# Attention scores and row maxima in one instruction stream: runs of 3, 3 and 2 pairs, one reduction over two PSUM banks for every other turn, and a lead of 28 turns in place of 30

## The reference

```python
q, k, v = (proj(wq, bq), proj(wk, bk), proj(wv, bv))
scores = jnp.einsum('bhqd,bhkd->bhqk', q, k) * scale
attn = jax.nn.softmax(scores, axis=-1)
out = jnp.einsum('bhqk,bhkd->bhqd', attn, v)
...
x = _layernorm(x + attention(x), axis=-1)
h = silu(tlin(x, w1)) * tlin(x, w2)
h = gelu(tlin(h, h1)); h = gelu(tlin(h, h2))
x = _layernorm(x + tlin(h, w3), axis=-1)
```

## Time and profile before

| what | value |
|---|---|
| median of 3 runs | 443.17 us (443.12 to 443.28) |
| span of the profiled execution | 441.5 us, first to last instruction |
| share of the span, PE / DVE / ACT / POOL | 97% / 88% / 83% / 20% |
| TensorE's granted clock | full speed in all 40 slices |

### The profile page before, as it was taken

The page is one execution under the profiler, slowest core; times in us unless marked ns, Lnnn a source line. Parts: engine busy times, 40 slices in busy tenths (PEclk is TensorE's granted clock), DMA queues, the critical chain, the costliest instruction groups (busy, mean ns, idle before and its releaser), DMA issues.

```text
span 441.5 us, 9824 instructions
## 1 busy us (share of the span) xinstructions
PE 427.8 (97%) x3496; PEld 227.0 (51%) x3498; DVE 386.5 (88%) x719; ACT 367.7 (83%) x694; POOL 90.3 (20%) x142
## 2 busy tenths in 40 slices
PE   8999999999999999999999999999899899999995
PEld 4543544444444444444444443544333488877884
DVE  6799999999999999999999999999884577657636
ACT  4487989998998999989899899999899886678762
POOL 9730000100000010000001002373311263046103
PEclk9999999999999999999999999999999999999999
DMA  6567741111130110113011001021021000000101
GB/s 165 176 196 129 270 147 33 44 28 28 48 122 25 45 31 28 27 48 122 25 46 33 26 27 49 14 43 47 15 39 50 13 8 1 1 2 2 48 1 48
DMA packets 17117, 24.88 MB, mean 56 GB/s; under 512 B 5169, under 2 KB 9009, under 8 KB 16689
## 3 DMA queue, kind: packets, MB, share of 16 engines
q1 hardware_dynamic: 16464, 23.68, 19.3%
q10 hardware_dynamic: 608, 0.59, 0.5%
HBM read 15.08 MB, written 7.60 MB: 51 GB/s over the span
## 4 chain that ended last, share of the span: by engine, by line
PE 76%; DVE 10%; ACT 5%; SPq 3%; DMA 2%; issue 2%; POOL 0%; POOLq 0%; DVEq 0%; ACTq 0%
PE ps L1369 24%; PE ps L1291 20%; PE ps L1479 16%; DVE negmax L977 9%; PE ps L1353 8%; ACT arena L664 2%; DMA parts_q<-arena 2%; PE ps L1223 2%; PE ps L1234 1%; PE ps L1423 1%; PE ps L1319 1%; PE ps L1263 1%; SPq L463 1%; SPq L435 1%; ACT v_pad L722 1%
## 5 line engine op out<-in xcount | busy, mean ns | idle before, releaser
L977 DVE TENSOR_REDUCE negmax<-ps 128x1 f32<-128x512 f32 x458 | 275.8, 701 | 1.8 <-PE ps L1291 1.5
L664 ACT ACTIVATE arena<-ps 128x512 f32<-128x512 f32 x360 | 190.0, 606 | 19.3 <-PE ps L1353 14.1
L1353 PE MATMUL ps<-qx,kx 64*128 64x512 f32 x512 | 171.3, 451 | 0.9 <-DMA qx<-mT 0.6
L1291 PE MATMUL ps<-kx,qx 61*128 61x512 f32 x468 | 160.2, 441 | 0.6 <-DMA qx<-parts_q 0.5
L1291 PEld LDWEIGHTS ps<-kx,qx 61*128 61x128 f32 x468 | 75.1, 184 | 88.6 <-DVE negmax L977 79.3
L1369 PE MATMUL ps<-arena,v_pad 128*32 128x256 f32 (+3 forms) x1328 | 104.8, 407 | 2.8 <-ACT arena L664 2.8
L664 ACT ACTIVATE hf<-ps 128x512 f32<-128x512 f32 x152 | 83.2, 604 | 9.4 <-PE ps L1353 8.4
L1353 PEld LDWEIGHTS ps<-qx,kx 64*128 64x128 f32 x512 | 78.9, 184 | 18.6 <-ACT arena L664 11.8
L1479 PE MATMUL ps<-hid,w_high 128*128 128x512 f32 (+1 forms) x296 | 68.3, 388 | 0.8 <-issue 0.4
L1479 PEld LDWEIGHTS ps<-hid,w_high 128*128 128x128 f32 x296 | 54.2, 188 | 12.3 <-issue 0.8
L1369 PEld LDWEIGHTS ps<-arena,v_pad 128*32 128x32 f32 x1328 | 28.5, 108 | 37.1 <-issue 30.7
(11 more groups left out here) (107 smaller groups left out, 317.2 us busy)
## 6 DMA issues: line engine op xcount, KB each, us to landing
qx<-parts_q SPq DMA_DIRECT2D x60, 64.0 KB, 2.1
late_sb<-in_late SPq DMA_DIRECT2D x3, 1280.0 KB, 5.5
kx<-parts_k SPq DMA_DIRECT2D x56, 64.0 KB, 2.2
parts_q<-prt SPq DMA_DIRECT2D x3, 512.0 KB, 6.4
parts_q<-arena SPq DMA_DIRECT2D x3, 512.0 KB, 8.3
xT_sb<-in_xT SPq DMA_DIRECT2D x4, 256.0 KB, 4.2
xT_sb<-arena SPq DMA_DIRECT2D x28, 32.0 KB
prt<-den SPq DMA_DIRECT2D x7, 128.0 KB
```

Of the source, the lines that this page charges most:

```text
L664: nc.scalar.activation(probs(n // HG)[:, heads(n), :], ps[:, PLAN["score", n][0], :], ACT.Exp, scale=SCALE).then_inc(exp_done, 1)
L977: nc.vector.tensor_reduce(negmax[:, t // TURNS % 2, m % 2, h * QT + q:h * QT + q + 1], ps[:, MAX_BANK + m % 4, :], AX.X, ALU.max, negate=T ...
L1291: nc.tensor.matmul(ps[:, half_bank(m), :], qx[at, slot, qc, h, q * P:(q + 1) * P], kx[at, slot, h, part * C:(part + 1) * C], start=True, s ...
L1353: nc.tensor.matmul(ps[:, bank, :], kx[at, slot, h % PAIR, kt * P:(kt + 1) * P], qx[at, slot, qc, h % PAIR, :], start=True, stop=True)\
```

## The change

Runs get three, three and two pairs in turn, so that three runs make eight pairs and two whole steps. On VectorE, the two halves of every even turn are reduced by one operation over two banks (`turn_both`), the halves of odd turns by one each as before. LEAD goes from 14 to 12: 25 turns in place of 27 in the beginning, and maxima 28 turns ahead of the scores. Plans that depend on run numbers are worked out from the new sizes.

```diff
-LEAD = 14
+LEAD = 12
...
-RUN_COLS = C * RUN // HG
-RUNS = (2 * U_ALL * TURNS - AHEAD + RUN - 1) // RUN
-TAIL = (RUN * (RUNS + RUN_BEFORE)) // HG
+PAIR_COLS = C // HG
+RUN_SIZES = (RUN, RUN, RUN - 1)
+BEFORE = RUN * RUN_BEFORE
...
+def run_at(g):
+
+    if g < 0:
+        return RUN * g
+    return g // len(RUN_SIZES) * sum(RUN_SIZES) + sum(RUN_SIZES[:g % len(RUN_SIZES)])
...
+def run_of(i):
+    return next(g for g in range(-RUN_BEFORE, i + 1) if run_at(g + 1) > i)
...
+RUNS = run_of(2 * U_ALL * TURNS - AHEAD - 1) + 1
+TAIL = (run_at(RUNS) + BEFORE) // HG
 GROUPS_ALL = RUNS + STEPS_ALL - (TAIL - 1)
-TURN_AT = {min((2 * TURNS * (w + 1) - 1 - AHEAD) // RUN + 3, RUNS + 1): w for w in range(1, U_ALL)}
+TURN_AT = {min(run_of(2 * TURNS * (w + 1) - 1 - AHEAD) + 3, RUNS + 1): w for w in range(1, U_ALL)}
...
-    return range(AHEAD + RUN * g, min(AHEAD + RUN * (g + 1), 2 * U_ALL * TURNS)) if g < RUNS else range(0)
+    return range(AHEAD + run_at(g), min(AHEAD + run_at(g + 1), 2 * U_ALL * TURNS)) if g < RUNS else range(0)
...
-    c0, c1 = RUN_COLS * g, RUN_COLS * (g + 1) if g < RUNS - 1 else (TAIL - 1) * C
+    c0, c1 = PAIR_COLS * run_at(g), PAIR_COLS * run_at(g + 1) if g < RUNS - 1 else (TAIL - 1) * C
...
+            def turn_both(i, m):
+
+                dve.wait_ge(max_scores, i * (2 * PER * TURNS) + m + 2)
+                t, bank = m // 2, MAX_BANK + m % 4
+                h, q = head_of(t % (PER * TURNS) + PER * TURNS)
+                nc.vector.tensor_reduce(negmax[:, t // TURNS % 2, 0, h * QT + q:h * QT + q + 1],
+                                        ps[:, bank:bank + 2, :], AX.XY, ALU.max, negate=True)\
+                  .then_inc(max_taken, 2)
...
                 for m in range(m0, m1):
-                    turn_half(i, m)
+                    if m % 4 == 0:
+                        turn_both(i, m)
+                    elif m % 4 > 1:
+                        turn_half(i, m)
```

More of the change, by code:

```diff
@@ L98, in scores_of @@
     if g < RUNS:
-        return range(RUN * (g + RUN_BEFORE), min(RUN * (g + RUN_BEFORE + 1), TAIL * HG))
+        return range(run_at(g) + BEFORE, min(run_at(g + 1) + BEFORE, TAIL * HG))
     k = g - RUNS + TAIL - 1
@@ L209, in half_bank @@
 def half_bank(m):
-    return MAX_BANK + (m + 2 * (FOLD // 2 + 1) if m < 2 * FOLD else m) % 4
+    return MAX_BANK + (m + WHOLE + 4 - FOLD if m < 2 * FOLD else m) % 4
 def build(nc, xT, wqT, wkT, wvT, woT, bq, bk, bv, bo, late,
@@ L283, in probs @@
             if k >= TAIL:
-                return probs_2[:, (k - TAIL) % 2]
+                return probs_2[:, (k - TAIL + TAIL % 3) % 2]
             return hf if k % 3 == 2 else probs_2[:, k % 3]
```

## The result

The changed kernel takes **458.48 us** (median of four runs, 456.98 to 461.05) against 443.14 us beside it: 1.0354 times as long (95% interval 1.0317 to 1.0390). The forecast of slower held; its 449.5 us and its range up to 454.5 us did not. The profiled execution took 456.98 us, its span is 455.2 us, 13.7 more than before.

The account below looks back on a forecast made before the run. VectorE bounds the kernel before; TensorE would bind after, at 19.70 us a unit. 13.44 units give +6.1 and the transposition +0.2, so 443.2 + 6.3 = 449.5 us, range 442.5 to 454.5.

Parts of the forecast that it names:

- TensorE passes VectorE: Main stretch: TensorE's unit rises from 18.8 to 19.40 us before late releases, above VectorE's 18.76 after the change.
- the short run: TensorE's third run of each block, with two pairs: takes 1.23 us, against 1.69 and 1.72 for three pairs.
- the unit's start: First product of a unit waits for ScalarE's copy and exponential: 0.58 us on TensorE, now in every unit.
- the transposition: Once a unit on TensorE it adds 0.26 us; at the end, up to 0.2 us behind the wait it stood in.
- the lead: Beginning: two folded turns less buy nothing, the score of unit 1 still waits until 56.23; four more halves remain.
- Every sign: Profile after: VectorE idle 0.2 us per block, blocks 4.7 to 4.8 and 5.2, record 1.22, first score 56.2, end 3.2.
- 13.44 x 19.70 = 264.8 against 258.7: Main stretch: units to go times us per unit, against the stretch measured before: +6.1 us, 2.4 from four further halves.
- of oddments: Main stretch: 0.14 us a unit, as VectorE has now, counted only in the upper bound of 20.05 a unit.
- The late release: Merged reduction frees its bank late for the next run's second pair: 0 to 0.17 us, taken as 0.10, 0.3 a unit.
- The end is the last reduction plus a constant: From last reduction through `norm` to `out_proj` and behind it nothing changes, except up to 0.2 us for the transposition.
- VectorE stays the bound: Rival for the main stretch: TensorE's unit falls below some 18.9, giving -4.5 us, 438.7 us; chance 0.15.
- The merged reduction costs its whole 1.225: Rival: no overlap, so VectorE keeps 19.5 a unit, 19.9 to 20.1 with unit starts; 452 to 454.7 us; chance 0.15.

Follow-up runs that it names:

- the runs alone: Changed kernel with LEAD back at 14 and every half reduced by itself, so only the 3, 3, 2 run plan differs from the kernel before: 447.44 us, 1.0102.
- the wait filled: Changed kernel with nine small identity matmuls while TensorE waits for `norm` ahead of `out_proj`: 456.68 us, 1.0302.
- the copy behind the exponential: Changed kernel with ScalarE's copy of a finished unit put behind the first exponential of the next run: 459.16 us, 1.0369.
- the merge in the first run: Changed kernel with LEAD 14 and merged reductions only in the first run of each block of eight pairs: 451.02 us, 1.0191.
- lead alone: Kernel before with LEAD 12 in place of 14, runs of three pairs and no merged reductions: 447.11 us, 1.0104.
- the kernel with the old lead: Changed kernel with LEAD put back from 12 to 14, keeping runs of 3, 3, 2 and merged reductions: 451.00 us, 1.0175.
- the two with half of the merges: Changed kernel with LEAD 14, merging only in each block's first run (451.02 us) or only in its second (447.72 us).

## Why the direction was right and the size was wrong

**Right.** TensorE passes VectorE: shown by the idle times and by the runs alone, whose pace (19.39) is the forecast's sum for TensorE without late releases (19.40). The parts of it in the changed kernel: the short run 1.23 (1.23 forecast); the unit's start 0.61 a block (0.58), now in every unit; the transposition 0.17 (0.26), since its block takes 4.97 against 4.80. The merged reduction has a record of 1.218 us and the next one begins 1.13 behind it (153.04 and 154.17). The rows of unit 1 landed at 56.15 (before 56.23), its first score began at 56.29, and the lead bought nothing in front. From the last maximum to `out_proj` it was a constant. Every sign that the prediction named came true: blocks of 4.80 and 5.25, a record of 1.22, 56.2 and 3.2.

**The step that failed** is the sum "13.44 x 19.70 = 264.8 against 258.7". The measured stretch is 270.99 us (56.15 to 327.14), 6.2 more. Of these, 4.8 are a comparison of unlike things and 1.5 a term that was too small.

- **A clean unit was set against a mean that wasn't clean.** At its pace of 19.22 the 13.31 units of before make 255.9 us, so the 258.7 hold 2.8 us of disturbances, 1.4 of them in the three late units. The 264.8 hold none; 0.14 a unit "of oddments" stood in the upper bound alone. The measured stretch is 4.8 us above 13.44 units at 19.81 (266.2): 2.8 in the three late units; 1.1 at the end, where 8 halves take 6.10 us and 8/32 of 19.81 is 4.95, since the unit's start among them makes a run of 2.84 in place of 2.33; and 0.8 in front, where 6 halves, from 56.15 to the copy of unit 0, take 4.54 and the pace gives 3.71, since the run that waits for the rows is held up. Even had all disturbances stayed as before, the stretch would have been 2.8 above the sum; that they grew by 2.0 was foreseen by no step.
- **The late release: "I take 0.10, between the ends".** It is 0.16 three times a unit, 0.48 in place of 0.30. The step before it was already wrong: by its own figures the load is 2.12 - 1.80 = 0.32 late and the matmul 2.12 - 2.03 = 0.09, and "0 to 0.17" follows from neither. The measured load is 0.32 late (0.43 behind the run's start in place of 0.11). A unit is then 18.56 + 0.48 + 0.61 + 0.17 = 19.82, measured 19.81, and not 19.70. That makes the 1.5 us.
- **"The end is the last reduction plus a constant."** The constant held up to `out_proj`. Behind it the forecast had 0.2 us for the transposition, and it is 1.5 us more.

**What no step had.** The prediction saw that one step leaves the wait for `norm`, and counted it as neither won nor lost. It made TensorE idle for 2.66 us there, and the clock behind that is 1.1 of the 1.5 us; that it is the idle time is shown by filling it. These terms (6.2 in the stretch, and 1.5 in place of 0.2 behind `out_proj`) lead from 449.5 to the profiled run's 456.98. The last 1.5 us are in the median: the other three runs of the change have mean clocks of 0.992, 0.986 and 0.992 against the profiled run's 0.995, and lie up to 4.1 above it. With the wait filled all four have 0.998 or 0.999 and lie within 1.1 us. But the four runs with the copy behind the exponential, whose wait is not filled, all have 0.992 and lie within 1.4, so why the change's runs spread so far is not shown.

**The rivals.** "VectorE stays the bound" is out: it idles 11.3 us in the main stretch. "The merged reduction costs its whole 1.225" is out by the 1.13, though its figure, 452 to 454.7, was nearer than mine, by luck: its reason did not hold. The rule of grouping on a saturated engine (the Trainium skill, Perfetto Trace Analysis, Optimizing Scalar/DVE Operations) was tested where it should be at its best, in the kernel before with a merge in twelve halves: the operations did get cheaper, by 0.07 to 0.09 a merge, and the kernel got slower. By the page's figure (an estimate) it would have been 0.125. The same section's other sentence, that breaking up may help where an unsaturated engine makes bubbles on another, agrees with the merge in the first run: without it the pace falls from 19.73 to 19.40.

**What stays open.** How much of the late units' loss goes if the weight work is moved away from the splits. What the other 0.4 us behind `out_proj` are, the moved transposition or something else: the runs alone have them too (123.78 against 123.34), at full clock. And no kernel has the new runs and 28 turns of lead without a merge.

## What to carry to other kernels

When two engines are both within a few per cent of full, work out the pace of each in a clean period, and compare clean with clean; put the disturbed periods and the ends in as terms of their own. An operation that takes two buffers at once starts later and gives both back later, so its price is in its neighbour's waits: look at who asks for the first of these buffers next, and merge only where that one comes late anyway (here the second run, at no cost, and no gain). And a fixed cost per group of work (here 0.31 us for each run: three pairs take 1.69 us and two take 1.23, so a pair 0.46, and 1.69 - 3 x 0.46 is left) is paid again for every group that a neater plan adds. Look also at what else is placed by counting such groups, as the weight work is here: it moves with them.

## What the runs showed of the hardware beyond what was expected

**TensorE's clock behind a wait of 2.7 us.** In six kernels, TensorE's idle time in front of `out_proj`, the mean granted clock from 320 to 340 us, and from `out_proj` to the end:

| kernel | idle before `out_proj` | clock | `out_proj` to the end |
|---|---|---|---|
| before | 0.86 | 1.00 | 123.34 |
| runs alone | 0.56 | 1.00 | 123.78 |
| lead alone | 2.68 | 0.91 | 124.86 |
| changed | 2.66 | 0.91 | 124.86 |
| changed, copy behind the exponential | 2.67 | 0.83 | 125.8 |
| changed, wait filled with matmuls | 0.48 | 1.00 | 123.8 |

All three with some 2.7 us idle had the lower clock behind it, one of them for about twice as long, and lost 1.1 to 2.0 us against the filled one or 1.5 to 2.5 against the kernel before. A shorter idle time did it once: the 1.65 us ahead of a late transposition, in the kernel with the old lead (0.79 from 284 to 292 us), while three kernels with 1.65 or 1.66 us at that place kept the full clock.

**VectorE beside GpSimd.** A multiplication of 128x512 fp32 on VectorE (`norm`) takes 1.76 us when GpSimd's subtraction of 128x512 (1.28 us) has begun 0.07 or 0.08 before it, and 0.69 without. Moving GpSimd's behind it moved the contention: it then takes 1.66 itself, and VectorE's 128x4096 operation beside it 3.37 in place of 2.28. Which of the two pays hangs on who is first. In the changed kernel GpSimd begins at 328.48, 0.07 ahead of VectorE's 328.55, and VectorE's first operation takes 1.74. In the kernel with both parts and the old lead VectorE is 0.08 ahead, its first operation takes 0.70, and GpSimd's takes 1.74:

```profile
325.87 2.38 DVE L1052 TENSOR_TENSOR xT_sb<-xT_sb,prt 128x512 f32<-128x512 f32 x2 [1.22 <-POOL mpart L850]
325.95 1.74 POOL L872 TENSOR_TENSOR w_low<-late_sb,w_high 128x512 fp32r<-128x512 f32 x1
```

This is the 1.0 us between the last maximum and `out_proj` (2.18 against 3.20) that this kernel, the runs alone and the two with half of the merges have over the changed one. It also puts right the reading that the 3.20 is fixed: it is fixed only as long as GpSimd comes first.
